# A fixed-slot ring for the last gather stage of a graph network kernel: waits by constants in place of a relay on SyncE

## What is computed

```python
all_msg = jnp.einsum('nf,rfo->rno', h, weight)
msg = all_msg[rel_type, src] * norm
gate = jax.nn.sigmoid(all_gate[rel_type, src])[:, None]
msg = msg * gate
agg = jax.ops.segment_sum(msg, dst, num_segments=n_nodes)
return jax.nn.relu(agg)
```

## Time and profile before

| | us |
|---|---|
| median of the timed executions | 3281.6 (3278.43 to 3282.46, 3 runs) |
| span of the profiled execution | 3773.2 |
| the same above the median | 491.6 |
| attention's gathers, first to last start, in the profile | 221.4 to 1583.7 |
| the last stage's gathers, first to last start, in the profile | 2550.1 to 3697.5 |
| last matmul of the last stage starts, in the profile | 3747.3 |

### The profile page before, as it was taken

One profiled execution on the slowest core, in us unless ns is written; L12 is line 12 of the kernel. 1 busy time (PEld: TensorE's weight loads), 2 busy tenths in 40 slices (PEclk: granted clock), 3 DMA queues, 4 the chain that ended last, 5 costly groups with the idle time before them and its releaser, 6 DMA issues. The chain is left out here.

```text
span 3773.2 us, 52431 instructions
## 1 busy us (share of the span) xinstructions
PE 2896.0 (77%) x13207; PEld 1940.5 (51%) x13207; DVE 2133.7 (57%) x4604; ACT 963.3 (26%) x2525; POOL 1732.1 (46%) x1863
## 2 busy tenths in 40 slices
PE   6838888888888888869999999992655555555555
PEld 4525555555555555549998888871333333333332
DVE  6727776677767777768862222222544444444446
ACT  3513333333333333346663333330000000000000
POOL 2555655555555555433300000006466666666661
PEclk9968998899989999979999999995867677776678
DMA  4455666666666666533345444445233333333332
GB/s 151 147 166 164 196 192 193 181 192 189 194 188 190 192 191 195 160 114 99 99 136 210 187 186 188 187 178 164 69 91 92 92 92 92 91 91 92 92 92 88
DMA packets 233908, 557.07 MB, mean 148 GB/s; under 512 B 48498, under 2 KB 128454, under 8 KB 221095
## 3 DMA queue, kind: packets, MB, share of 16 engines
q0 software_dynamic: 104144, 324.24, 30.4%
q1 hardware_dynamic: 108463, 193.61, 14.1%
q10 hardware_dynamic: 21032, 35.85, 3.2%
HBM read 402.87 MB, written 150.71 MB: 147 GB/s over the span
## 5 line engine op out<-in xcount | busy, mean ns | idle before, releaser
L1294 POOL DMA_INDIRECT rel_rows<-msg_d,msg_i_again x783 | 743.3, 949 | 976.8 <-ACTq L1274 571.7
L1314 PE MATMUL rel_ps<-rel_rows,rel_hot 128*128 x1664 | 678.5, 538 | 525.0 <-issue 364.4
L873 POOL DMA_INDIRECT qv_rows<-qv_d,src_i x832 | 798.4, 960 | 567.6 <-PE out_ps L1155 354.2
L1314 PEld LDWEIGHTS rel_ps<-rel_rows,rel_hot 128*128 128x128 f32 x1664 | 367.1, 254 | 836.5 <-issue 806.3
L1339 DVE TENSOR_TENSOR sums_all<-sums_all,rel_ps 128x256 f32 x832 | 350.4, 421 | 630.4 <-PE rel_ps L1314 247.0
L1155 PE MATMUL out_ps<-qv_rows,hot 128*128 128x264 f32 x1664 | 635.8, 467 | 44.8 <-DVE qv_rows L950 25.0
L1031 ACT COPY at_acc<-out_ps 128x264 f32 x832 | 310.3, 380 | 726.9 <-PE out_ps L1155 581.1
L1110 PE MATMUL kx<-k,hot_t 128*128 x2496 | 398.4, 297 | 64.4 <-issue 48.4
L896 DVE TENSOR_TENSOR qv_rows<-qv_rows,kx 128x512 f32<-128x512 f32 x416 | 278.7, 679 | 204.4 <-remote 121.6
L1957 PE MATMUL up_hid_ps<-up_split,ms_hTs 128*128 128x512 f32 x1416 | 347.5, 396 | 0.0
L1110 PEld LDWEIGHTS kx<-k,hot_t 128*128 128x128 bf16 x2496 | 252.9, 105 | 175.4 <-issue 108.6
(11 more groups left out here) (213 smaller groups left out, 2883.3 us busy)
## 6 DMA issues: line engine op xcount, KB each, us to landing
msg_d<-up_x SPq DMA_DIRECT2D x33, 1024.0 KB, 3.9
msg_d<-up_gelu SPq DMA_DIRECT2D x33, 1024.0 KB, 3.8
msg_d<-up_res SPq DMA_DIRECT2D x32, 1024.0 KB, 3.8
dl_b<-dlt_d ACTq DMA_DIRECT2D x50, 512.0 KB
qv_rows<-qv_d,src_i POOLq DMA_INDIRECT x832
rel_rows<-msg_d,msg_i_again POOLq DMA_INDIRECT x783
qv_d<-qv SPq DMA_DIRECT2D x6, 1820.0 KB, 7.2
agg_d<-at_acc SPq DMA_DIRECT2D x49, 132.0 KB
```

The lines of the kernel that those rows point to most:

```text
L873: nc.gpsimd.indirect_dma_start(rows[:, n % SLOTS, :], None, qv_d, bass.IndirectOffsetOnAxis(ap=src_i[:, n:n + 1], axis=0)).then_inc(got[n ...
L1294: nc.gpsimd.indirect_dma_start(rows[:, at:at + FEAT], None, table, bass.IndirectOffsetOnAxis(ap=msg_i[:, e:e + 1], axis=0)).then_inc(got[e ...
L1314: nc.tensor.matmul(sum_ps[n % BANKS][:], hot[:, n % HOTS, :], rows[:, bass.ds(at, FEAT)], start=True, stop=True).then_inc(summed, 1)
```

## The change

The table now holds, per step, the address of the slot in a ring of 80: `prepare` works out the edge tile's number less 80 times its lap by five more small VectorE operations on a 52 x 16 table, and multiplies by 256. `rel_rows` grows from 64 to 80 slots (80 KB of each partition in place of 64). Each of the 20 semaphores `got` now stands for 4 neighbouring slots (`PER`), so a group's semaphore counts 4 gathers per lap. GpSimd no longer waits for landings; it waits, from gather 80 on, until step e - 31 is done. SyncE only loads `x1_all`. TensorE no longer asks for the tile that a step reads: at every fourth step n below 783 it waits, against a constant, until gathers up to n + 3 have landed, and it neither computes the remainder nor waits on a register.

```diff
+                    did(nc.vector.tensor_tensor(edge_of[:], step_of[:], window[:, QUAD:QUAD + UNROLL], ALU.subtract))
+                    did(nc.vector.tensor_scalar(lap_of[:], edge_of[:], 1.0 / LAST_SLOTS, 0.5 / LAST_SLOTS - 0.5, ALU.mult, ALU.add))
...
+                    nc.vector.tensor_scalar(tab[:, EDGES_AT:PLACES_AT], edge_of[:], float(FEAT), None, ALU.mult)
...
+    PER = LAST_SLOTS // len(got)
     before = [16 * len([n for n in range(STEPS) if n % SLOTS // 2 == b]) for b in range(len(got))]
+    landed = lambda last: len([e for e in range(last + 1) if e % LAST_SLOTS // PER == last % LAST_SLOTS // PER])
-    RING = 64
...
-                for e in range(DENSE):
-                    b = e % len(got)
-                    sp.wait_ge(got[b], before[b] + 16 * (e // len(got) + 1))
-                    sp.sem_inc(landed, 1)
                 sp.wait_ge(x1_ld, 16 * GROUPS)
...
                 for e in range(DENSE):
-                    if e >= RING:
-                        pool.wait_ge(summed, e - RING + NODE_TILES + 1)
-                    if e >= len(got) and e % 4 == 0:
-                        pool.wait_ge(landed, e - len(got) + 4)
-                    at = (e + 1) % RING * FEAT
+                    if e >= LAST_SLOTS:
+                        pool.wait_ge(summed, e - LAST_SLOTS + NODE_TILES + 1)
+                    at = e % LAST_SLOTS * FEAT
...
-                ahead = [edge_of(0), edge_of(1)]
+                ahead = [slot_of(0), slot_of(1)]
                 for n in range(STEPS):
-                    edge = ahead.pop(0)
-                    at = nc.s_assert_within(pe.snap(edge & (RING - 1)) * FEAT, 0, (RING - 1) * FEAT,
-                                            skip_runtime_bounds_check_because="the remainder of a division by the ring's length")
+                    at = ahead.pop(0)
+                    if n < DENSE and n % PER == 0:
+                        newest = min(n + PER, DENSE) - 1
+                        b = newest % LAST_SLOTS // PER
+                        pe.wait_ge(got[b], before[b] + 16 * landed(newest))
                     pe.wait_ge(hot_ok, n + 1)
-                    pe.wait_ge(landed, edge)
                     nc.tensor.matmul(sum_ps[n % BANKS][:], hot[:, n % HOTS, :], rows[:, bass.ds(at, FEAT)],
                                      start=True, stop=True).then_inc(summed, 1)
```

More of the change, by code:

```diff
@@ L73 @@
 DENSE = EDGE_TILES + 1
+LAST_SLOTS = 80
 K_PARTS = 3
@@ L236, in prepare @@
         step_of = sb(ctx, "step_of", [ROUNDS, UNROLL])
+        edge_of = sb(ctx, "edge_of", [ROUNDS, UNROLL])
+        lap_of = sb(ctx, "lap_of", [ROUNDS, UNROLL])
         wq = sb(ctx, "wq", [P, KC, 3 * FEAT])
@@ L352, in tables @@
                     nc.vector.tensor_tensor(same[:], window[:, QUAD + 1:], window[:, QUAD:QUAD + UNROLL], ALU.is_equal)
-                    nc.vector.tensor_tensor(tab[:, EDGES_AT:PLACES_AT], step_of[:], window[:, QUAD:QUAD + UNROLL], ALU.subtract)
+                    did(nc.vector.tensor_tensor(edge_of[:], step_of[:], window[:, QUAD:QUAD + UNROLL], ALU.subtract))
+                    did(nc.vector.tensor_scalar(lap_of[:], edge_of[:], 1.0 / LAST_SLOTS, 0.5 / LAST_SLOTS - 0.5, ALU.mult, ALU.add))
+                    did(nc.vector.tensor_scalar(lap_of[:], lap_of[:], U_ROUND, None, ALU.add))
+                    did(nc.vector.tensor_scalar(lap_of[:], lap_of[:], -U_ROUND, None, ALU.add))
+                    did(nc.vector.scalar_tensor_tensor(out=edge_of[:], in0=lap_of[:], scalar=-float(LAST_SLOTS), in1=edge_of[:],
+                                                       op0=ALU.mult, op1=ALU.add))
+                    nc.vector.tensor_scalar(tab[:, EDGES_AT:PLACES_AT], edge_of[:], float(FEAT), None, ALU.mult)
                     did(nc.vector.tensor_scalar(third[:], window[:], float(NODE_TILES), -float(OUT_BANKS), ALU.is_ge, ALU.mult))
@@ L607, in _ @@
                 nc.gpsimd.iota(part_c[:], [[IC, ICN]], base=0, channel_multiplier=1, **exact).then_inc(consts, 1)
-                nc.gpsimd.iota(step_of[:], [[1, UNROLL]], base=1, channel_multiplier=UNROLL, **exact).then_inc(consts, 1)
+                nc.gpsimd.iota(step_of[:], [[1, UNROLL]], base=0, channel_multiplier=UNROLL, **exact).then_inc(consts, 1)
                 nc.gpsimd.memset(ones[:], 1.0).then_inc(consts, 1)
@@ L1257, in edge_sum @@
 def edge_sum(nc, sb, ps, sem, table, sums, iota_n, late, place, msg_i, idx_ld, late_ld, x1_d, x1_all, got):
+    PER = LAST_SLOTS // len(got)
     before = [16 * len([n for n in range(STEPS) if n % SLOTS // 2 == b]) for b in range(len(got))]
+    landed = lambda last: len([e for e in range(last + 1) if e % LAST_SLOTS // PER == last % LAST_SLOTS // PER])
     BANKS = 4
     HOTS = 4
-    RING = 64
-    x1_ld, hot_ok, summed, acc_ok, zero_ok, landed = (
-        sem(f"rel_{n}") for n in ("x1", "hot", "sum", "acc", "zero", "landed"))
+    x1_ld, hot_ok, summed, acc_ok, zero_ok = (sem(f"rel_{n}") for n in ("x1", "hot", "sum", "acc", "zero"))
     with ExitStack() as ctx:
         dloc, norm_s = late[:, 0], late[:, 1]
-        rows = sb(ctx, "rel_rows", [P, RING * FEAT])
+        rows = sb(ctx, "rel_rows", [P, LAST_SLOTS * FEAT])
         hot = sb(ctx, "rel_hot", [P, HOTS, P])
@@ L1295, in _, with slot_of @@
                                                  bass.IndirectOffsetOnAxis(ap=msg_i[:, e:e + 1], axis=0)
-                                                 ).then_inc(got[e % len(got)], 16)
+                                                 ).then_inc(got[e % LAST_SLOTS // PER], 16)
             @block.tensor
             def _(pe):
-                def edge_of(n):
+                def slot_of(n):
                     r, s = n // UNROLL, n % UNROLL
                     return nc.values_load_multi_w_load_instructions(
-                        place[r:r + 1, s:s + 1], engines=[mybir.EngineType.PE], min_val=1, max_val=DENSE,
-                        skip_runtime_bounds_check_because="the tile of edges that a step reads, counted from one")[1][0]
+                        place[r:r + 1, s:s + 1], engines=[mybir.EngineType.PE], min_val=0, max_val=(LAST_SLOTS - 1) * FEAT,
+                        skip_runtime_bounds_check_because="the table holds the remainder of a division by the ring's length")[1][0]
@@ L1316, in _ @@
                     if n + 2 < STEPS:
-                        ahead.append(edge_of(n + 2))
+                        ahead.append(slot_of(n + 2))
             @block.vector
```

## The result

The changed kernel takes 3321.28 us (median of 4 executions, 3319.95 to 3323.28), the kernel before 3280.49 us (3278.43 to 3282.46). The ratio is 1.0127, 95% interval 1.0115 to 1.0139: 40.8 us slower. The forecast was 3324, which is 42.4 above the 3281.6 of the three runs then known.

What follows compares the result with a forecast made beforehand. The prediction took the timed last stage to be bound by POOL's issue of gathers, 981 us. It added 42 us of tail and 1 us of table to 3281.6, giving 3324.6, so 3324; range 3285 to 3332, chance 0.77.

Steps and rivals of the forecast that it cites:

- The budget: Whole kernel: both gather stages at gather pace, 1043 + 981 us, and a shorter end give 3241, 41 under the median.
- The 41 us that the budget left over: Median time above the 3241 us sum; given to attention, whose 1062 us of VectorE owes at least 19 of it.
- The rival that put those 41 us in the last stage: Last stage: late steps behind a full ring; ring 80 and shorter path repay the tail, 3282 to 3312; chance 0.10.
- PE is slow in the profile for that reason alone: Profile's last stage: PE's slowness comes only from data-free instructions stretched twentyfold while gathers stream; 3.5 us a step.
- the first rival: PE's sequencer, last stage: TensorE bounds timed runs too, so the change gains, 3197 at midpoint, 3280 near the floor; chance 0.08.
- The tail: End of last stage: 52 steps left behind the last landing, 50 more at 0.839 us each, +42 us (31 to 43).
- The terms at nothing: Last stage: GpSimd's dropped landing wait, ring 80, TensorE's saved sequencer work and the relay hop, each taken to gain nothing.
- The relay's hop: SyncE, between landing and step: one hop less, worth between 0 and 0.7 us, taken as 0.
- the 1 us for the table's five operations: VectorE in prepare: five more operations of about 0.16 us, each waited for; 0 to 2 us, taken as 1.
- The rule on shared ports: Last stage: one-hots would block gather descriptors, so moving 50 steps behind the gathers returns up to 17 us; not taken.
- The slower rival: Tail: PE stays at the lower clock, 1.2 GHz, so 52 steps cost 1.04 us each, 54 us, 3337; chance 0.05.
- The changed profile: Signs: gathers 1.254 us apart, at least 104 matmuls behind the last landing, at least 43 us to end, span 3640 to 3760.

Runs made afterwards that it cites:

- e10: Changed kernel with early waits only for steps 0 to 639, exact tile waits from 640, and SyncE's relay by groups of four; 3282.18 us, ratio 1.0010 to before.
- e7: The changed kernel run again without an edit, in a session of the upper level; 3765.99 us, before 3770.28, ratio 0.9984.
- e4: Changed kernel with TensorE's wait 16 gathers further ahead, so 68 steps instead of 52 stand behind the last landing; 3332.33 us, ratio 1.0165 to before.
- e1: The kernel before, run again without an edit for a second trace, at the upper level; 3796.28 us.
- e2: Kernel before with one edit: TensorE waits at every fourth step for gathers up to n + 3, not for the tile read; ratio 0.9977, upper level.

## Why the prediction was right, and where it was not

**What bounds the timed runs.** Right. The budget said that gathers pace both stages: 981 us forecast, 980.4 seen in the changed kernel and 978.2 in `e10` (3245.0 - 2266.8), whose time is that of before. The 41 us that the budget left over were given to attention: its gathers take 1080.4 us, 37 over their floor. The rival that put those 41 us in the last stage falls with that. That before itself has these gathers is inferred: no recording of it at the lower level exists.

**What the recording was.** Wrong in its cause. The prediction took the long span as something that the timed executions do not have. Those timed then did not; timed executions of other sessions do, at 3762 to 3801 us. "PE is slow in the profile for that reason alone", the stretched instructions, is wrong too: `e7` has 1.44 us a step without them. And of the 132.6 us of idle time of POOL that were read as waiting for PE, 175 x 0.30 = 53 us are the pause ahead of any gather; 76.0 us more (50 times) have `remote` as their releaser. The step held because it was made by a budget against the timed median and not by the belief. It follows that the cost of the change hangs on the level: 1.0127 at the lower, 0.9984 at the upper, where the first rival (TensorE is late anyway) has the place right but not the price. It counted 69 us of sequencer work and a stage down to 1028 us; 4 us were gained, and the stage kept its 1199.

**The tail.** Right in mechanism and size: 52 steps behind the last landing forecast, 104 matmuls seen; 0.84 us a step forecast, 44.1 / 52 = 0.85 seen; +42 for 50 of them forecast, +40.8 measured in all. The slope by `e4`, 0.78 to 0.88 us, and the 36.7 us that `e10` takes away say the same from both sides. One sum is off: 43 + 2 us above 3281.6 is 3327, not 3328, which changes nothing.

**The terms at nothing.** Gathers without the landing wait go 1.254 us apart, as the earlier trace rows has them with it. The ring of 80, the slot table, the missing register operation and GpSimd's missing wait together stay within what `e10` leaves, 1.0010. The relay's hop was taken as 0, and no run shows it by itself, as `e10` has a relay again; the 1 us for the table's five operations is too small to be told apart. One-hots beside gathers cost them nothing that shows: median 949 ns and 1.254 us from start to start over the last stage, where VectorE builds them, as in the earlier trace rows. The rule on shared ports, of the Trainium skill, "SBUF — State Buffer", in its note on the "DVE blocks DMA" trap, would, by the prediction's estimate, have given up to 17 us back when 50 one-hots moved behind the gathers; +40.8 beside a forecast of +42 without it leaves no room for that, and the gathers with one-hots beside them are no slower. Whether these one-hots run in a two-port mode at all no run shows.

**The slower rival.** The granted clock was 0.76 over the stretch in which TensorE waits for landings and 0.64 in the 3.9 us ahead of the tail, between its lower level (0.5, 1.2 GHz) and its upper one (1.00, 2.4 GHz). It did not stay there: over the 52 steps it was 0.92. A step took 0.85 us, not 1.04; VectorE's pace covers it.

**The changed profile.** The signs in the last stage came as named: gathers 1.254 us apart, 104 matmuls behind the last landing, 48 us from the last gather to the end of the additions. The span was wrong: 3640 to 3760 was forecast. It was 3321.5 in a session of the lower level and 3771.6 in one of the upper. The reason given, two instructions fewer to be stretched, fails on its own terms: nothing of TensorE's is stretched any more (37 ns), and the pace is the same 1.44 us.

## What to carry to other kernels

When consumers are faster than a stream of loads but have more steps than there are loads, the extra steps are free only if they run while loads are still coming; a wait that is simplified to a constant must be read for how many steps it leaves behind the last landing, and that number times the step's own pace is the loss. It need not be exact everywhere: exact waits in the last quarter of the stage's steps brought back nine tenths of it. Before a recording's durations are used against a timed median, compare the two spans; where they differ by 15%, a budget of the stages by their floors tells which waits the timed runs can have. None of the three versions timed at the lower level (the changed kernel, `e4`, `e10`) beats the kernel before.

## What was not expected of the hardware

The same program takes 3278 us in one session and 3801 us in another, each within 0.4% there, and the numbers given for the chips do not sort the two: chip 1 gave both. (One execution of `e2` took 6276 us; why is not known.) At the upper level only the two stages with gathers are longer (attention 1371.1 us of gathers in `e1` for 1080.4 in the changed kernel's recording, the last stage 1159.2 for 980.4; between the two stages it is 967.2 for 967.6), each gather still takes its 0.95 us, and TensorE and VectorE start up to four us after what they need is there, as long as gathers go out. After the last gather they do not: the tail of `e7` runs at 64.8 / 77 = 0.84 us a step. The expectations call these late signals; that the signals are late, and not the instructions that wait for them, is not shown, nor is either shown to be the cause.
